# Row-range preparation on Pool and rank counting inside the layernorm of a one-core GNN kernel

## The reference

```python
h = jnp.maximum(_layernorm(x, axis=-1), 0.0)
msg = jnp.concatenate([h[dst], edge_attr], axis=1)
msg = jnp.maximum(msg @ W1a + b1a, 0.0) @ W1b + b1b
summed = jax.ops.segment_sum(msg, src, num_segments=6250)
counts = jax.ops.segment_sum(jnp.ones(200000), src, num_segments=6250)
agg = summed / jnp.maximum(counts, 1.0)[:, None]
out = x + jnp.maximum(jnp.concatenate([h, agg], axis=1) @ W2a + b2a, 0.0) @ W2b + b2b
```

## Time and profile before

| | |
|---|---|
| median of 3 runs | 1596.23 us (1592.51 to 1596.64) |
| profiled execution, its own time | 1601.71 us |
| its span in the profile | 1600.0 us |
| busy: PE, PEld | 1469.5 us (92%), 1401.1 us (88%) |
| busy: DVE, ACT, POOL | 1419.4 us (89%), 1025.4 us (64%), 1203.0 us (75%) |
| transfers | 186.56 MB, mean 117 GB/s |

### The profile page before, as it was taken

One profiled execution on the slowest core, in us unless ns is written; L12 is line 12 of the kernel. 1 busy time (PEld: TensorE's weight loads), 2 busy tenths in 40 slices (PEclk: granted clock), 3 DMA queues, 4 the chain that ended last, 5 costly groups with the idle time before them and its releaser, 6 DMA issues.

```text
span 1600.0 us, 77513 instructions
## 1 busy us (share of the span) xinstructions
PE 1469.5 (92%) x31132; PEld 1401.1 (88%) x31132; DVE 1419.4 (89%) x4789; ACT 1025.4 (64%) x2192; POOL 1203.0 (75%) x794
## 2 busy tenths in 40 slices
PE   4378999999999999999999999999999999999936
PEld 3267999999999999999999999999999999999924
DVE  7857998999989999898899999998989999999937
ACT  5167666766676666666667666676667666666403
POOL 5267877778787777887887787778877877778771
PEclk8689999999999999999999999999999999999967
DMA  5666766666666666676676766776767667667551
GB/s 164 240 119 107 124 110 109 121 108 114 116 110 118 108 121 113 110 119 108 111 121 111 123 109 109 121 113 109 124 110 121 110 108 125 110 114 118 80 132 45
DMA packets 278692, 186.56 MB, mean 117 GB/s; under 512 B 190215, under 2 KB 274692, under 8 KB 277569
## 3 DMA queue, kind: packets, MB, share of 16 engines
q1 hardware_dynamic: 173358, 152.31, 38.2%
q0 software_dynamic: 104976, 29.30, 25.9%
HBM read 147.32 MB, written 34.17 MB: 113 GB/s over the span
## 4 chain that ended last, share of the span: by engine, by line
PE 86%; DVE 5%; issue 3%; ACT 2%; POOL 2%; DMA 1%; DVEq 0%; SPq 0%; POOLq 0%; ACTq 0%
PE l_ps L1267 39%; PE l_ps L1253 22%; PE z_ps L1218 12%; PE c_ps L1242 5%; PE z_ps L1230 3%; PE z_ps L1223 3%; ACT area L708 1%; DMA xs<-in_x 1%; POOL sums L531 1%; DVE rank L880 1%; POOL xs L621 0%; DVE area L961 0%; DMA sums<-vv,sidx 0%; DVE oh L946 0%; ACT r_d L691 0%
## 5 line engine op out<-in xcount | busy, mean ns | idle before, releaser
L531 POOL DMA_INDIRECT sums<-vv,sidx x726 | 1155.3, 1591 | 336.4 <-issue 169.4
L1267 PE MATMUL l_ps<-area 128*128 128x64 bf16 (+1 forms) x21000 | 767.3, 193 | 12.3 <-issue 4.7
L1267 PEld LDWEIGHTS l_ps<-area 128*128 128x128 bf16 x21000 | 729.8, 98 | 34.7 <-issue 21.6
L708 ACT ACTIVATE area<-l_ps 64x392 bf16<-64x392 f32 x1400 | 684.5, 489 | 84.5 <-PE l_ps L1253 62.5
L961 DVE TENSOR_SCALAR area<-iota,local 128x640 bf16<-128x640 int16 x1400 | 481.1, 408 | 4.9
L1253 PE MATMUL l_ps<-r_d,oh 128*128 128x196 bf16 x4200 | 480.6, 249 | 2.2 <-ACT area L708 1.3
L1253 PEld LDWEIGHTS l_ps<-r_d,oh 128*128 128x128 bf16 x4200 | 343.5, 96 | 15.7 <-ACT area L708 2.7
L946 DVE TENSOR_SCALAR oh<-iota,rank 128x640 bf16<-128x640 int16 x846 | 285.3, 404 | 0.0
L691 ACT ACTIVATE r_d<-z_ps 128x384 f32<-128x384 f32 x423 | 207.5, 491 | 83.4 <-PE z_ps L1223 71.4
L696 ACT ACTIVATE vv<-c_ps 128x396 f32<-128x396 f32 x121 | 60.6, 500 | 253.8 <-PE c_ps L1242 244.9
L968 DVE TENSOR_TENSOR dense<-l_ps,dense 128x325 f32<-128x325 f32 x280 | 136.7, 488 | 93.9 <-PE l_ps L1267 93.2
(11 more groups left out here) (133 smaller groups left out, 731.6 us busy)
## 6 DMA issues: line engine op xcount, KB each, us to landing
ids_s<-ids SPq DMA_DIRECT2D x246, 192.0 KB
et_d<-in_e_t SPq DMA_DIRECT2D x143, 192.0 KB
ids_d<-ids SPq DMA_DIRECT2D x143, 192.0 KB
et_s<-in_e_t SPq DMA_DIRECT2D x123, 192.0 KB
sums<-vv,sidx POOLq DMA_INDIRECT x726
sums<-dense POOLq DMA_DIRECT2D x3, 1657.5 KB
wp_d<-p_table SPq DMA_DIRECT2D x286, 15.8 KB
wp_s<-p_table SPq DMA_DIRECT2D x246, 15.8 KB
```

Source lines behind the costliest of these rows:

```text
L531: nc.gpsimd.indirect_dma_start(out=sums[t][:, :], out_offset=bass.IndirectOffsetOnAxis(ap=index, axis=0), in_=rows, in_offset=None, comput ...
L708: ins = nc.scalar.activation(routed[on, t.div(MACRO).mod(2), first:second + 1:second - first, t.mod(MACRO), :], bank[on, :, :], ACT.Copy)
L1267: ins = nc.tensor.matmul(l2_ps[h][:, u * W:u * W + w], oh2[:, g, u * P:(u + 1) * P], rows[:, PARTS[r]:PARTS[r] + w], start=g % MACRO == 0 ...
```

## The change

- VectorE loses lane, column, bucket, masks, places and bases. Pool does them: lane, column, bucket and the masks ahead of its layernorm stages, places and bases behind its transfers of zeros. Two fused operations become two each, since Pool multiplies and subtracts in separate instructions. Pool waits for itself by `pool_step`.
- The copy of the source numbers (`srcf`) moves from ACT to the start of Pool's run.
- `row_i` moves away from the masks: `dst` rows behind `iota_i`, `src` rows into `dense`. So the clearing of `dense` moves behind the cast of the `src` rows.
- TensorE counts bucket b inside the layernorm, at the step of turn b + 3, in banks `l2_ps` and `c_ps` in place of `l2_ps` and `l1_ps`, and VectorE's predicated copies follow `p_keep` of the same turn. The product of `W1b` and `W2a`, which uses `c_ps[0]`, comes after the ranks.
- ACT casts `earlier_b` at the start.
- `pipelined` writes out every step; no loop remains in it, in the layernorm or in the last stage.

```diff
@@ -209,7 +209,6 @@
 
         ROWW = ROWG * SUB * P
         ids_s = sb("ids_s", [P, SR, 2, GE], i16)
-        row_i = [words(k * ROWW, ROWW, ROWP).bitcast(i32) for k in range(2)]
         row_16 = [ids_s[0:ROWP].rearrange("p s a e -> p (s a e)")[:, k * ROWW:(k + 1) * ROWW] for k in range(2)]
         masks = words(0, BUCKETS * DT // 2).bitcast(bf16).rearrange("p (b k g) -> p b k g", b=BUCKETS, k=TPG)
         n_masks = BUCKETS * DT // 2
@@ -217,6 +216,7 @@
         at = n_masks + NTP * 3 * D // 2
         bucket = words(at, DT)
         iota_i = words(at + DT, LOCAL).bitcast(i32)
+        row_i = [words(at + DT + LOCAL, ROWW, ROWP).bitcast(i32), dense[0:ROWP, 0:ROWW].bitcast(i32)]
         earlier = at_st[:, 0, 0:P]
         sq = at_st[:, 1, :], hid_st[:, 0, :]
         lane, column = (oh1[:].rearrange("p k c -> p (k c)").bitcast(f32)[:, k * DT:(k + 1) * DT] for k in range(2))
...
+
+                def step(ins):
+
+                    steps[0] += 1
+                    ins.then_inc(pool_step, 1)
+                    pool.wait_ge(pool_step, steps[0])
+
+                pool.wait_ge(src_in, 16)
+                nc.gpsimd.tensor_copy(srcf[:], ids_i).then_inc(src_ready, 1)
+                pool.wait_ge(src_ready, 1)
+                source = srcf[:, 0:DT].rearrange("p (g k) -> p k g", k=TPG)
+                middle = -(NT - 1) / 2 / NT
+                step(nc.gpsimd.tensor_scalar(by_tile(lane), source, 1.0 / NT, middle, ALU.mult, ALU.add))
+                step(nc.gpsimd.tensor_scalar(lane, lane, SHIFT, SHIFT, ALU.add, ALU.subtract))
+                step(nc.gpsimd.tensor_scalar(column, lane, float(NT), None, ALU.mult))
+                step(nc.gpsimd.tensor_tensor(by_tile(column), source, by_tile(column), ALU.subtract))
+                step(nc.gpsimd.tensor_scalar(bucket, column, 1.0 / UNITS, -(UNITS // 2) / UNITS, ALU.mult, ALU.add))
+                step(nc.gpsimd.tensor_scalar(bucket, bucket, SHIFT, SHIFT, ALU.add, ALU.subtract))
+                pool.wait_ge(row_ready[0], 1)
+                for b in range(BUCKETS):
+                    nc.gpsimd.tensor_scalar(masks[:, b, :, :], by_tile(bucket), float(b), None, ALU.is_equal).then_inc(masks_ready, 1)
                 pool.wait_ge(rows_in[1], 16)
                 nc.gpsimd.tensor_copy(row_16[1], row_i[1]).then_inc(row_ready[1], 1)
...
@@ -520,12 +537,23 @@
                     pool.wait_ge(mid_ready, done(m + 1))
                     nc.gpsimd.tensor_tensor(of_turn(m, 2), xc[:, bass.ds(m * NPG, NPG), :], of_turn(m, 1), ALU.subtract).then_inc(low_ready, 1)
 
-                pipelined(pool, [(1, rest), (0, low)])
+                pipelined([(1, rest), (0, low)])
 
                 pool.wait_ge(zeros_ready, 1)
                 for k in range(TABLES):
                     zero(k)
                 pool.wait_ge(consts_ready, CONSTS)
+                step(nc.gpsimd.tensor_scalar(place[:, side[1]], bucket[:, side[1]], 0.5, -0.25, ALU.mult, ALU.add))
+                step(nc.gpsimd.tensor_scalar(place[:, side[1]], place[:, side[1]], SHIFT, SHIFT, ALU.add, ALU.subtract))
+                step(nc.gpsimd.tensor_scalar(place[:, side[1]], place[:, side[1]], 4.0, None, ALU.mult))
+                step(nc.gpsimd.tensor_tensor(place[:, side[1]], place[:, side[1]], bucket[:, side[1]], ALU.subtract))
+                nc.gpsimd.tensor_scalar(place[:, side[0]], bucket[:, side[0]], float(PLACES), 1.0, ALU.mult, ALU.add).then_inc(places_ready, 1)
+                nc.gpsimd.tensor_scalar(place[:, side[1]], place[:, side[1]], float(PLACES), float(PLACES + 1),
+                                        ALU.mult, ALU.add).then_inc(places_ready, 1)
+                pool.wait_ge(base_in, 16)
+                step(nc.gpsimd.tensor_scalar(basew[:], base_i[:], 1.0 / 3, None, ALU.mult))
+                step(nc.gpsimd.tensor_scalar(basew[:], basew[:], SHIFT, SHIFT, ALU.add, ALU.subtract))
+                nc.gpsimd.tensor_scalar(basew[:], basew[:], wlane[:, 0:1], None, ALU.add).then_inc(places_ready, 1)
 
                 def scatter_rows(k, t, index, rows):
                     nc.gpsimd.indirect_dma_start(
...
                 nc.scalar.activation(row_16[0], row_i[0], ACT.Copy).then_inc(row_ready[0], 1)
 
+                act.wait_ge(consts_ready, CONSTS)
+                nc.scalar.activation(earlier_b[:], earlier, ACT.Copy).then_inc(ident_b_ready, 1)
                 act.wait_ge(ones_ready, 3)
...
-                act.wait_ge(src_in, 16)
-                nc.scalar.activation(srcf[:], ids_i, ACT.Copy).then_inc(src_ready, 1)
+                pipelined([(3, h_keep), (7, square), (6, root), (1, high), (0, mid)])
+
                 act.wait_ge(src_ready, 1)
-                act.wait_ge(consts_ready, CONSTS)
-                nc.scalar.activation(earlier_b[:], earlier, ACT.Copy).then_inc(ident_b_ready, 1)
                 nc.scalar.activation(src_t[:], srcf[:], ACT.Identity, bias=untrash[:]).then_inc(src_ready, 1)
...
+                def rank(b, m):
+
+                    n = m - (NTURNS - BUCKETS)
+                    if n < 0:
+                        return
+                    dve.wait_ge(ranks_raw, n + 1)
+                    if n:
+                        dve.wait_ge(ranks_kept, n)
+                    for k, bank in enumerate(rank_ps[n % 2]):
+                        chosen = masks[:, n, k * SUB:(k + 1) * SUB, :].rearrange("p k g -> p (k g)").bitcast(mybir.dt.uint16)
+                        ins = nc.vector.copy_predicated(pos[:, side[k]], chosen, bank[:, 0:SUB * DG])
+                    ins.then_inc(ranks_kept, 1)
+
+                pipelined([(2, norm), (3, rstd), (4, square_sum), (5, centre), (6, row_sum), (0, p_keep), (0, rank)])
 
...
                 dve.sem_inc(wides_ready, 1)
+                dve.wait_ge(places_ready, 3)
                 step(nc.vector.tensor_tensor(pos, pos, place, ALU.add))
-                dve.wait_ge(base_in, 16)
-                step(nc.vector.tensor_scalar(basew[:], base_i[:], 1.0 / 3, None, ALU.mult))
-                step(nc.vector.tensor_scalar(basew[:], basew[:], SHIFT, SHIFT, ALU.add, ALU.subtract))
-                step(nc.vector.tensor_scalar(basew[:], basew[:], wlane[:, 0:1], None, ALU.add))
                 dve.wait_ge(fits_raw, 1)
...
+                def count(bank, at, weights, b, k, n, start=False):
+
+                    return nc.tensor.matmul(bank[:, at * DG:(at + n) * DG], weights,
+                                            masks[:, b, k:k + n, :].rearrange("p k g -> p (k g)"),
+                                            start=start, stop=True, skip_group_check=True)
+
+                def counts(_, m):
+                    b = m - (NTURNS - BUCKETS)
+                    if b < 0:
+                        return
+                    if b == 0:
+                        pe.wait_ge(ident_b_ready, 1)
+                    pe.wait_ge(masks_ready, b + 1)
+                    if b > 1:
+                        pe.wait_ge(ranks_kept, b - 1)
+                    for k, bank in enumerate(rank_ps[b % 2]):
+                        count(bank, 0, earlier_b[:], b, k * SUB, SUB, start=True)
+                        for before in range(1, SUB):
+                            ins = count(bank, before, ones_b[:], b, k * SUB, SUB - before)
+                    ins.then_inc(ranks_raw, 1)
+
                 pe.wait_ge(w_in, 16)
-                pipelined(pe, [(1, transposes), (0, p_rows)], straight=True)
-
+                pipelined([(1, transposes), (0, p_rows), (1, counts)])
+
+                pe.wait_ge(ranks_kept, BUCKETS)
                 nc.tensor.matmul(c_ps[0][:, 0:P], wts[:, C_W1B_T:C_W1B_T + P], wts[:, C_W2A_BOT:C_W2A_BOT + P],
                                  start=True, stop=True)
                 nc.tensor.matmul(c_ps[0][:, P:P + 1], wts[:, C_W2A_BOT:C_W2A_BOT + P], wts[:, C_B1B:C_B1B + 1],
...
```

81 lines of the change are left out of this document (15 added, 66 removed).

## The result

| | kernel before | changed kernel |
|---|---|---|
| median of 5 runs each | 1595.63 us (1590.25 to 1596.64) | 1617.89 us (1616.51 to 1620.44) |
| ratio to before, 95% interval | | 1.0147 (1.013 to 1.0164) |
| profiled execution | 1601.71 us, span 1600.0 | 1618.17 us, span 1616.4 |
| Pool's first "rest" (T0) | 23.96 us | 60.11 us |
| Pool's last "low" ends (P) | 46.3 us | 83.9 us |

The changed kernel is slower by 22 us, 1.5%. The forecast was 1602.4 us with a range of 1593 to 1612: the direction was right, the time lies outside. Between the two profiled executions the span differs by 16.4 us: the start is 25.5 us later, the last stage 5.2 us shorter, and the edge loop, which is the same in both, took 4.0 us less (1455.1 against 1459.1 us).

The account below looks back on a forecast made before the run. TensorE's edge loop was taken as the bound, a later start carrying through one for one. First edge matmul at 68.8 + 24.3 = 93.1 us (+7.2), last stage 1 us less: +6.2, so 1602.4 us, range 1593 to 1612.

Parts of the forecast that it names:

- the price of a one-input step on Pool: Pool's run before its first "rest": each one-input operation on 846 columns takes 0.95 us, bounded by 0.79 and 1.83.
- Rival (b): Pool's run before T0: one-input steps cost 1.83 us like two-input ones, +19.4 us, 1615.6; with prices up to it 17%.
- The port: Shared by VectorE and Pool: VectorE's two-input operations wait until Pool pauses, none in the masks; Pool put back 1.8 + 0.4 us.
- Behind T0: Rest of the layernorm after Pool's first "rest": turns of 3.2 us in steps 3 to 6, 28.1 us in all, P at 68.8.
- Rival (a): Pool's run before T0: quick one-input steps (0.75 us) and a free port, T0 35.3, P 59.2, 1592.7 us; chance 15%.
- P + 24.3: First edge matmul after Pool's last layernorm operation: dense windows in at P + 21.6, then 2.7 us of TensorE work.
- the dear end: VectorE's work after Pool's places and bases ends between P + 13 and P + 18; at P + 18 it comes out even.
- The last stage: Written-out loops at the kernel's end save 0 to 0.2 us a turn over ten turns, 0 to 2 us; 1 taken.
- The removal from VectorE: VectorE's start-up stretch shrinks by well over 10 us but no longer sets the end; worth what the new P leaves.

## Why the prediction was right in sign and wrong in size

**The step that failed is the price of a one-input step on Pool.** The sum took 0.95 us for each of fifteen (five steps and ten masks), from the casts, and bounded it by 0.79 and 1.83. Measured, from the first timeline above:

| term | predicted | measured |
|---|---|---|
| sources in | 15.3 | 15.47 |
| copy of 1680 columns | 1.56 | 1.58 |
| five one-input steps (lines 511, 512, 513, 515, 516), stride included | 5.05 | 11.26 |
| two-input step, one input strided | 1.83 | 2.67 |
| ten masks | 9.5 | 23.74 |
| cast, memset | 4.7 | 4.69 |
| waiting at the port | 2.2 | none told apart (the two-input step may hold 0.2 to 0.3) |
| gaps between its instructions | 0.5 | 0.7 |
| T0 | 40.7 | 60.11 |

The one-input steps account for 6.2 + 14.2 = 20.4 us and the two-input step for 0.8; the port gives 2.2 back. The two-input step reads the sources with a stride, for which the sum had added nothing there; Pool's two-input step of line 549, on 423 columns without a stride, took 1.07 us, where the 2.16 ns a column of the earlier trace rows make 0.91. Two of the five, the multiply-adds, came out at 0.96 and (strided) 1.67 us, so the choice of 0.95 was right for that form. The error was to treat "one input" as the kind: the casts of the earlier trace rows are copies, and a copy shares its price with a multiply-add alone. Even the dear bound, the two-input add, was too low for the comparison, which takes 2.37 us against 1.83. Rival (b) named the place and not the mechanism: it let all one-input steps cost 1.83 us, where the multiply-adds keep the price of the casts and the rest cost more than that. Its 1615.6 us is the nearest of the four to 1617.9, and that is luck: it has T0 6.2 us and the first edge matmul 5.1 us too early and the last stage 4.2 us too long. In the Trainium skill, "GPSIMD Engine Reference", section "Elementwise — side-by-side cycle accounting", a body of up to two operations runs at 1.03 cycles an element; the estimate was 0.73 us for 846. The trace agrees for the multiply-add to within 0.2 us (0.91), and not for a comparison (2.37) or a single add (2.56), where the measurement decides.

**The port.** The prediction held VectorE at step 2 of the layernorm until the masks ended. It did not stay there. While Pool's add-subtract of line 512 ran, from 18.90 to 22.04 us, VectorE's operations on two SBUF inputs came through, one in 0.71 us and two at full speed, and so did one in the midst of the masks (38.32 us). The two-input step of line 514 held one of them for 2.21 us, as the earlier trace rows had shown for a cast.

```profile
19.41 0.71 DVE L841 SCALAR_TENSOR_TENSOR xc<-stat,xs 128x256 f32<-128x256 f32 x1
...
20.37 0.41 DVE L856 TENSOR_TENSOR stage<-xc,stat 128x256 f32<-128x256 f32 x1
...
21.19 0.41 DVE L841 SCALAR_TENSOR_TENSOR xc<-stat,xs 128x256 f32<-128x256 f32 x1
...
25.32 2.21 DVE L841 SCALAR_TENSOR_TENSOR xc<-stat,xs 128x256 f32<-128x256 f32 x1
...
38.32 0.41 DVE L856 TENSOR_TENSOR stage<-xc,stat 128x256 f32<-128x256 f32 x1
```

VectorE then filled its pipeline as far as Pool's missing results allow, into step 3.

**Behind T0** the layernorm took 83.9 - 60.1 = 23.8 us, where the prediction had 28.1. That VectorE stood a step further brought little of it: the next `p_keep` came 3.5 us after T0, against 1.0 + 3.2 in the sum. The turns were shorter.

```profile
63.59 0.41 DVE L862 TENSOR_TENSOR xc<-z_ps,rowb 128x256 f32<-128x256 f32 x1
...
66.42 0.41 DVE L862 TENSOR_TENSOR xc<-z_ps,rowb 128x256 f32<-128x256 f32 x1
```

A full turn took 2.83 us in place of 3.2. The prediction took 1.22 for a pair of predicated copies from a stretch in which VectorE also waits 0.10 us between pairs; here a pair puts the next operation off by 1.03, and the rest of the turn takes 1.80 in place of 1.96. From 63.59 to the last `p_keep` at 80.95 that is 17.4 us against 21.1. Rival (a), a free port, had 23.9 behind T0, but from step 4 on with turns of 2.96; so the match is in part luck. Its other half, quick steps, was wrong.

**P + 24.3.** It was P + 27.5 (27.8 to 28.2 in three other kernels). The prediction had the zeros at P + 16.3 and the windows of the dense kind at P + 21.6, read from where the transfers were through in a trace in which nobody waited for them. In the changed kernel the first one-hot after the zeros came at P + 17.8, the dense identities released VectorE at P + 21.1 and the sparse windows TensorE at P + 22.0, and behind the dense identities stood VectorE's own chain of 6.4 us to the edge matmul (105.01 to 111.44; in the kernel before 79.53 to 85.95). The prediction had hung that chain on the zeros alone and put only TensorE's 2.7 us behind the loads: P + 21.1 + 6.4 is the 27.5. Between P + 13 and P + 18 the prediction had VectorE's work behind places and bases end. Pool was done with them at 97.54 us (P + 13.6): they took 11.8 us behind the issue of the zeros, where the sum had 5 to 10, again for their lone and add-subtract forms. VectorE's part then ended, with the gap before the one-hots, at P + 17.8: the dear end, at which it comes out even, as the prediction had said of it.

**The last stage.** The mechanism was right and the size was not: 1 us was predicted, at most 2, and 5.2 measured (4.7 with the loops alone). The prediction put 0 to 0.2 us of a turn of 2.93 to loop and register work. The turns of the loop are 2.77 and 2.93 us by turns, and became 2.50. Start and last stage errors in sum: T0 +19.4, behind it -4.3, behind P +3.2, last stage -4.2, together +14.1 of the 15.5 us between forecast and median; the rest is within what two medians and two loops differ by.

**The removal from VectorE** was worth nothing, as predicted, since P took over. What was missed there is that the part of it which doesn't delay P, lanes and places, does gain (3.4 us at the start with the loops, of which the loops alone give 1.7), and that masks and counts inside the layernorm's turns, which the prediction did not price apart, put the first edge matmul 7.0 us later than masks and counts behind them. Which of the two costs more was not run by itself; in a turn, a pair of copies takes VectorE 1.03 us, and a mask with what it does to `norm` 1.0.

## What to carry to other kernels

Price an operation for GpSimd by its form as well as its width and number of inputs: in these runs, on 846 columns, a fused multiply-add costs what a copy does, while a comparison, a lone add or multiply, or an add-subtract costs two and a half to three and a half times that (the lone multiply four times beside VectorE's own work), and the rounding by a large constant is cheaper as two multiply-adds than as one add-subtract. Before moving work off the engine that ends last, find the event that everything else hangs from (here P, with 24 to 28 us of transfers and first work behind it), and put nothing ahead of it that can stand behind it. When that event moves, each wait that was hidden becomes one, so the work behind it has to be counted from the later event on, not from where it ended before.
